# Pooling steps after the bounds and sums of h, the first sum of h in another place, one product ahead by one

## The reference

```
h      = gelu(x @ fc1_w.T + fc1_b)                  # 512 -> 2048
shared = h @ fc2_w.T + fc2_b                        # 2048 -> 384
expert = h @ experts_w[indices[b]].T + experts_b    # 2048 -> 128, weights chosen per batch
x      = x + concat(shared, expert)
scores = tanh(x @ W1 + b1) @ v
p      = softmax of the scores over the tokens that a mask (prefix, postfix or cloze) leaves
x      = x + (p @ x) / count
```

## Time and profile before

| what | value |
|---|---|
| median of 3 runs | 1432.12 us (1429.52 to 1435.58) |
| the profiled execution | 1433.8 us, of which its span 1431.7 us |
| PE busy | 1328.0 us (93%) |
| DVE busy | 1073.7 us (75%) |
| ACT busy | 968.6 us (68%) |
| POOL busy | 271.7 us (19%) |
| mean granted clock of PE | 0.971 |

### The profile page before, as it was taken

The page is one execution under the profiler, slowest core; times in us unless marked ns, Lnnn a source line. Parts: engine busy times, 40 slices in busy tenths (PEclk is TensorE's granted clock), DMA queues, the critical chain, the costliest instruction groups (busy, mean ns, idle before and its releaser), DMA issues.

```text
span 1431.7 us, 25597 instructions
## 1 busy us (share of the span) xinstructions
PE 1328.0 (93%) x9849; PEld 974.8 (68%) x9849; DVE 1073.7 (75%) x2092; ACT 968.6 (68%) x1764; POOL 271.7 (19%) x380
## 2 busy tenths in 40 slices
PE   9999999989989899898998989989899798997998
PEld 4457484757768577685776857768577685775855
DVE  7888897758678676786767867677676686766898
ACT  5769678575856758577685766857658476584772
POOL 0000101211222112221222212222221221122201
PEclk9999999999999999999999999999999999999999
DMA  7630223253352533534335343453434434335306
GB/s 276 190 83 15 46 82 67 67 125 75 97 110 71 121 81 97 104 82 111 81 99 102 84 108 82 108 96 83 109 79 110 91 86 105 82 96 104 69 17 118
DMA packets 73885, 136.43 MB, mean 95 GB/s; under 512 B 9747, under 2 KB 34211, under 8 KB 71331
## 3 DMA queue, kind: packets, MB, share of 16 engines
q0 software_dynamic: 28032, 56.63, 22.9%
q1 hardware_dynamic: 45154, 77.38, 16.4%
q10 hardware_dynamic: 576, 0.79, 0.2%
HBM read 45.65 MB, written 18.87 MB: 45 GB/s over the span
## 4 chain that ended last, share of the span: by engine, by line
PE 69%; DVE 16%; DMA 9%; ACT 3%; issue 2%; POOL 1%; POOLq 0%; DVEq 0%; ACTq 0%
PE ps L649 12%; PE ps L547 12%; PE ps L549 11%; PE ps L548 11%; DMA hl<-hl 8%; PE ps L657 4%; PE ps L660 4%; PE ps L636 3%; PE ps L638 3%; PE ps L637 3%; DVE xl L1619 2%; DVE hl L1662 1%; DVE hl L1619 1%; ACT L1199 1%; DVE space L2064 1%
## 5 line engine op out<-in xcount | busy, mean ns | idle before, releaser
L547 PE MATMUL ps<-xh,w1h 128*128 128x256 f16 x960 | 261.7, 273 | 0.0
L549 PE MATMUL ps<-xh,w1l 128*128 128x256 f16 x960 | 261.7, 273 | 0.0
L548 PE MATMUL ps<-xl,w1h 128*128 128x256 f16 x960 | 261.7, 273 | 0.0
L1035 ACT ACTIVATE g<-ps,b1s,ds 128x512 f32<-128x512 f32 x240 | 173.3, 773 | 65.5 <-PE ps L549 65.5
L547 PE MATMUL ps<-xh,ch 128*128 128x256 f16 x720 | 196.4, 273 | 0.0
L549 PE MATMUL ps<-xh,cl 128*128 128x256 f16 x720 | 196.2, 273 | 0.0
L548 PE MATMUL ps<-xl,ch 128*128 128x256 f16 x720 | 196.2, 273 | 0.0
L1619 DVE SCALAR_TENSOR_TENSOR hl<-g,ix,hh 128x512 f16<-128x512 f32 x243 | 176.1, 745 | 3.1
L1009 ACT ACTIVATE hh<-g,ix 128x512 f16<-128x512 f32 x243 | 161.6, 719 | 0.0
L1009 ACT ACTIVATE ps<-ps 128x256 f32<-128x256 f32 x192 | 71.3, 371 | 94.5 <-PE ps L660 57.0
L649 PE MATMUL ps<-hh,w 128*128 128x512 f16 x576 | 134.1, 379 | 0.0
(11 more groups left out here) (364 smaller groups left out, 3183.6 us busy)
## 6 DMA issues: line engine op xcount, KB each, us to landing
space<-in_xT SPq DMA_DIRECT2D x62, 256.0 KB, 3.2
g<-space SPq DMA_DIRECT2D x60, 256.0 KB, 3.5
er<-in_ew SPq DMA_DIRECT2D x15, 1024.0 KB, 4.9
out<-space SPq DMA_DIRECT2D x60, 256.0 KB, 3.2
space<-space POOLq DMA_DIRECT2D x52, 256.0 KB, 3.3
hl<-hl POOLq DMA_DIRECT2D x24, 512.0 KB, 7.7
g<-space POOLq DMA_DIRECT2D x30, 256.0 KB, 4.1
g<-g POOLq DMA_DIRECT2D x30, 256.0 KB, 3.3
```

What stands on the lines that cost most here:

```text
L547: mm(to, wh, mh, start=i in (1, 5) and c == 0, stop=False, skip_group_check=True)
L548: mm(to, wh, ml, start=False, stop=False, skip_group_check=True)
L549: m = mm(to, wl, mh, start=False, stop=c == 1, skip_group_check=True)
L1035: act(in_two(g_of(b, k)), src, ACT.Gelu, bias=b1s[:, k:k + 1], scale=ds1[:, b % 2, p:p + 1]).then_inc(gelu_done)
```

## The change

In `vector_program` the pooling steps of a paired batch are given out as 2, 3, 7, 3 and 2 instead of 9, 4 and 4. They follow `bounds`, `third_sum` and `batch_scales` with what hangs on them, instead of standing ahead. `first_sum` writes T1 to `h[1, FIRST]`, over T3, and leaves T2 as it is. So it waits for the expert's product 7 and no longer for the POOL transfers; product 5 reads the new place, and `split_x2_high`, which overwrites `h[1, SECOND]`, also waits for the expert's product 3. The static product 5 goes ahead of the expert's 3. `fourth_sums` moves into `sum_quarters`, ahead of the transfer into T4, and waits for the second sum alone. On ACT the split of T4 moves into the opening and `inverses` up by one. In the opening `product3` goes ahead of `score`. At the start SP's first puts wait for the low part of w2's second chunk.

```diff
-    H_OF = {1: (FIRST_K, 0), 6: (FIRST_K, 0), 5: (FIRST_K, 0), 7: (FIRST_K, 1),
+    H_OF = {1: (FIRST_K, 0), 6: (FIRST_K, 0), 5: (FIRST_K, 1), 7: (FIRST_K, 1),
...
-               (STATIC, 3), (EXPERT, 3), (STATIC, 5), (STATIC, 4), (EXPERT, 5), (EXPERT, 4))
+               (STATIC, 3), (STATIC, 5), (EXPERT, 3), (STATIC, 4), (EXPERT, 5), (EXPERT, 4))
...
         def sum7(b, v):
-            e.wait_ge(s_step, s_value(b, E3_DONE if v == EXPERT else T3_HIGH))
-            e.wait_ge(moved, t3_low_moved(b))
+            e.wait_ge(s_step, s_value(b, E3_DONE if v == EXPERT else T2_DONE))
...
+            sum5(b, STATIC)
             sum3(b, EXPERT)
-            sum5(b, STATIC)
...
+            product3(n, 0)
             score(b)
-            product3(n, 0)
...
         def split_x2_high(b, c):
+                e.wait_ge(s_done, nth_product(b, EXPERT, 3))
...
             split_x2_high(b, ROW)
+            split_x_high(n, T4)
             fifth_copy_of_sum(b, EXPERT)
...
+                inverses(b - 1)
                 third_of_sum(b, EXPERT)
-                inverses(b - 1)
                 split_x_high(b + 1, T2)
                 split_x_high(b + 1, X22)
-                split_x_high(b + 1, T4)
...
         def first_sum(b, h):
-            e.wait_ge(s_done, nth_product(b, EXPERT, 6))
-            e.wait_ge(moved, all_moved(b))
-            tt(y, y, x, ALU.subtract).then_inc(s_step)
+            e.wait_ge(s_done, nth_product(b, EXPERT, 7))
+            tt(h[:, 1, FIRST_K, :], y, x, ALU.subtract).then_inc(s_step)
...
                 expert_sum2(b)
-                pool(9)
+                pool(2)
                 bounds(b + 1)
                 third_sum(b)
+                pool(3)
                 second_sum(b, hh)
                 second_sum(b, hl)
                 batch_scales(b + 1)
                 expert_sum3(b)
                 add_left(b, STATIC)
                 add_left(b, EXPERT)
-                pool(4)
+                pool(7)
                 first_sum(b, hh)
                 first_sum(b, hl)
                 x_low(b + 1, X11)
                 x_low(b + 1, X21)
+                add_row(b, STATIC)
                 x_low(b + 1, T3)
                 x_low(b + 1, T1)
-                add_row(b, STATIC)
...
+                add_row2(b, EXPERT)
                 x2_low(b, ROW2)
-                add_row2(b, EXPERT)
                 add_first(b + 1, 0)
                 x2_low(b, 3)
+                x2_low(b, 0)
                 add_second(b + 1, 0)
-                x2_low(b, 0)
-                pool(4)
+                pool(3)
                 attention_low(b)
                 add_first(b + 1, 1)
+                pool(2)
...
+        e.wait_ge(w2l_done, nth_chunk(1, 3))
         put_quarters(1)
...
         def fourth_sums(b):
-            e.wait_ge(s_step, s_value(b, E2_DONE))
+            e.wait_ge(s_step, s_value(b, T2_DONE))
...
             add_quarters(b, T2, g[:, PLACES.index(T3), :])
+            if paired(b - 1):
+                fourth_sums(b - 1)
             e.wait_ge(*combined_by(b, T2))
             add_quarters(b, T4, g[:, PLACES.index(T2), :])
```

More of the change, by code:

```diff
@@ L2645, in fourth_sums @@
             e.wait_ge(s_done, nth_product(b, EXPERT, 2))
-            e.wait_ge(s_step, s_value(b, E2_DONE))
+            e.wait_ge(s_step, s_value(b, T2_DONE))
             eng.dma_start(ee[:, 1].rearrange("p a k n -> p (a k n)"),
                           expert_sums[b % 2][:, 1].rearrange("p a k n -> p (a k n)"), accum_op=ALU.add).then_inc(moved, 16)
-            e.wait_ge(s_step, s_value(b, T2_DONE))
             for h in (hh, hl):
@@ L2673, in gpsimd_program @@
             sum_quarters(n + 1)
-            if paired(n):
-                fourth_sums(n)
             mend(n - 1)
```

## The result

The changed kernel takes 1351.0 us, the median of 4 runs (1350.62 to 1351.38), against 1433.32 us for the kernel before (4 runs, 1429.52 to 1435.58): a ratio of 0.9428, 95% interval 0.9406 to 0.945. The forecast was 1356 within 1342 to 1384.

What follows compares the result with a forecast made beforehand. PE, busy 93% of the span, bounds the kernel, so its idle and slow time is the gain: 126.4 us removed less 50.6 new, net 75.8 off 1433.8, gives 1358.0, less 1.7 for the median: 1356 us, range 1342 to 1384.

Steps and rivals of the forecast that it cites:

- Part 1: PE's `mx` wait in paired batches: bounds ahead of seven pooling steps removes 61.8 us and 27.6 us of slow clock.
- Part 2: Second sum of h, late next: PE idles 1.5 us for hh and 0.25 for hl, 1.75 us a batch.
- Part 3: First sum, behind seven pooling steps: PE idles 1.5 us at static 5 and 0.25 at its low half.
- Part 4: POOL transfers into `hl`: 19.9 us of waits go, 5 come, including 0.2 a batch for T4's transfer.
- The 17 us that I put beside it: POOL transfers: loss if T4's transfer slowed those issued before it by a full 1.6 us a batch.
- Part 5: Opening: waits for the last row add and `attention_low` go, 13.5 us; 3.6 us of new wait for `keep_score`.
- the term for `keep_score`: Opening, score one product later: 0.25 to 0.3 us of new wait, 3.6 us in all.
- Part 6: Start, SP's four puts moved later: effect between -1.4 and +1.5 us, taken as 0.
- A: PE's corrections: new stalls lower the clock once a batch, 28 us more, 1384 us; chance 0.12.
- B: Expert 3: T4's transfer or the earlier start costs 1.6 us or more a batch, 1373 us; chance 0.12.
- C: ACT: T4's split delays the expert's fifth copy if its transfer lands past 603.6; slower, 1457 us at 612; chance 0.04.
- D: Chain product waits for something else, so 12 x 5.15 stay; within 7 us of 1432; chance 0.04.

Runs made afterwards that it cites:

- bounds-late kernel: The changed kernel with all nine pooling steps ahead of `bounds` again: 1398.83 us, ratio 0.976 to the kernel before.
- the fastest kernel: The changed kernel with both second sums before the exponentials' pooling step, four steps before the first sum, score before product 3, own semaphore for expert weights' transfer: 1302.67 us.
- the kernel with the old order: The changed kernel with expert product 3 ahead of static product 5 again, the first sum keeping its new place: 1391.32 us.
- the second sum ahead of the exponentials: The changed kernel with both second sums of h ahead of the pooling step that waits for ACT's exponentials: 1334.98 us.
- the kernel with T4's transfer first: The changed kernel with POOL's transfer into T4 of g ahead of the fourth sums again: 1351.82 us.
- bounds alone: The kernel before with only `bounds` moved, after two pooling steps with the other seven directly behind: 1398.82 us.
- bounds alone with the transfer held back: The kernel before with `bounds` moved ahead and the transfer of expert weights held until the second sum is done: 1425.71 us.
- the one with the old place and order: The changed kernel with the first sum over T2 again, waiting for all fourth-sum transfers, and expert product 3 ahead of static 5: 1393.23 us.

## Why the prediction was right

The answer was, the mechanism was, and the size was within 7 us, in part because errors cancelled. Point by point, by its parts.

**Part 1, bounds ahead: right.** `mx` was forecast ready four us before PE wants it, and is (558.53 against 562.51). The bounds-late kernel brings back exactly the 61.8 us. The slow clock went in full: 29.3 us by the granted clock over PE's busy time, where the sum had 27.6 + 3.6 = 31.2. It took batch 6's 2.3 us for all twelve stalls, and in batches 12 and 14 the slow stretch was half as long.

**Part 2, the second sum as the next late thing: right.** Forecast 1.5 and 0.25, measured 1.43 and 0.27. It is read off the same queue of DVE: the step that needs the exponentials, then the sum.

**Part 3, the first sum: right.** Forecast 1.5 and 0.25, measured 1.45 (0.52 in the last batch) and 0.27. Parts 2 and 3 together: 42 us forecast, 33.6 + 6.4 = 40.0 measured.

**Part 4, POOL's transfers: right in size, with one wrong step in it.** The wait is 1.6 us in three batches (0.19, 0.20 and 1.18), where 5 us stood in the sum, 2.4 of them a price for T4's transfer on the fourth sums (its "own run of about 1.6" stands in no row). The chain from the second sum to the landing takes 10.6 us in batch 6, as forecast. The price was zero, because the step that had T4 issued right behind the others was wrong: POOL held the transfer back for 7.66 us, until all of them had landed. The Trainium skill ("DMA: Bandwidth & Descriptors", "Issuing engines are not separate DMA queues") has all transfers share 16 engines and interleave. The 17 us that I put beside it did not come, and the changed kernel does not test the rule, since T4's transfer never ran beside the fourth sums. In the fastest kernel it does, which agrees with the rule, and there the late one pays: in batch 6 the fourth sums of hh and hl land 7.0 and 8.9 us after their issue in both kernels, while T4's takes 6.1 us instead of 3.5 (6.1 to 7.7 over the twelve batches, against 3.2 to 4.6). That the order of the products makes this cover was in the prediction ("thanks to static 5 going ahead"), but not what it is worth with the rest in place: 40 us.

**Part 5, the opening: mis-sized.** Both waits went, 13.5 us. The new gaps are 2 x 0.29 x 12 = 7.0 us, where the term for `keep_score` was 3.6: the step stopped at the first product that waits for `keep_score`, and left out ACT's next first copy, which stands behind it. It also left out what the removed wait was made of: in the attend part before there was a second gap of 0.21 us a batch, too short to be listed, 2.5 us in all, and it went too.

**Part 6, the start: 1.3 us gained,** inside its bounds of -1.4 to +1.5. Taking the wait away gives about 1 us back.

**The sum.** Ahead of each listed wait the last matmul counts as busy for 0.27 us, where the pace is 0.11: 0.16 us of tail each, for 46 waits before and 27 after, 3.1 us less. Removed 61.8 + 29.3 + 19.9 + 13.5 + 2.5, 1.3 at the start and 3.1 of tails are 131.4. New 33.6 (the listed stalls), 1.6 for the transfers, 7.0 in the opening and the 6.4 of low halves are 48.6. The difference is 82.8, and the spans differ by 82.1. Against the forecast of 75.8 the missing 7 us are 3.4 of transfers that cost nothing, 2.0 of smaller stalls, and 2.5, 1.3 and 3.1 not counted or taken as 0, less 1.9 of clock and 3.4 of a second gap. The lower bound of the range does not follow from the terms named for it: without T4's price (2.4) and half of the second and third parts' idle (21) the time is 1356 - 23, so 1333 and not 1342; for 1372 no working is given. The time measured lies in the range either way.

**The rivals.** *A, the new stalls keep the clock low:* not in the changed kernel. All 24 stalls (1.43 to 1.46 us, the last one 0.52) were followed by full pace. The rule of the Trainium skill that stood beside it ("TensorE: Matmul & The Clock Gate", "A second HAM failure mode: psum-queue depth-cycling") did not decide in this kernel. A was closer than its 0.12 sounded, however: in the kernel with the old order, the six waits of 2.31 to 2.65 us all lowered the clock, and with the second sum ahead of the exponentials two waits of 2.11 and 2.15 did. *B, POOL's transfers become the wait:* did not happen, yet the same kernel shows how near it was; with one product less of cover they are 36.1 us. *C, T4's split on ACT:* PE lost nothing by it, but one of the signs that the prediction named as wrong came: ACT waited for T4's transfer in its opening, in batches 3, 4 and 12 (0.88, 0.34 and 0.40 us). I had T4 issued at once, and it was held back by 7.66 us; against C I also gave 10.6 us as the slowest chain from the second sum to PE, which is batch 6's, where the slowest of before is 12.1. What was left is 1.45 us in batch 6, in which ACT waits for PE ahead of the fifth copy at 583.95, and 0.46 in batch 3. *D, it does not do what it says:* excluded by the `mx` rows. Its price was wrong: the bounds-late kernel keeps the whole stall with the rest of the change and takes 1398.83 us, and not 1432 within 7.

## What to carry to other kernels

When a stall is taken away, work out for every later consumer both times again: when the producer is done and when it is now wanted. Whoever forgets the second (as I did with the first sum, after the stall ahead of it went) sees the stall move on and not go. An edit can be worth nothing by itself and much together with another, as the free place with the product that may then go ahead: cost such pairs as a pair, and look for work that may run in the shadow of a transfer before trying to shorten the transfer. Gaps too short for the list of waits were found here by comparing row starts with the pace, and count twelve times all the same.

## What the runs showed of the hardware

**An issue that waits for earlier transfers.** POOL stood for 7.66 us ahead of issuing a 256 KB adding transfer, until the third of three 512 KB adding transfers had landed (POOL's rows of the changed kernel); in all twelve batches the issue starts 0.26 us after that landing. In the fastest kernel, where the first of the three signals another semaphore, the same issue stood for 2.57 us only, until that first one had landed (issued at 551.88, 4.9 us to landing, and the next issue at 557.07). Again the distance from that landing is 0.26 us in all twelve batches:

```profile
551.88 0.85 POOL L2653 DMA_DIRECT2D ee<-expertsums  x1 [3.80 <-DVE hl L1732]
...
557.07 0.87 POOL L2661 DMA_DIRECT2D g<-g  x1 [2.57 <-issue]
```

In the kernel with T4's transfer first, the issue of the fourth sum of hh stands for 1.29 us in batch 6 and comes 0.26 us after T4's has landed, with a single other transfer then in flight, where the changed kernel has three. So a plain limit on how many are in flight does not explain it. What holds the issue back was not settled: no run changes the number or size of the transfers by itself. For a plan it means that an adding transfer's place in POOL's order can delay it by the whole landing time of those ahead of it, and POOL's own next work with it.

**The clock after a stall does not follow from its length alone.** Waits of 5.1 us were followed by the 1.2 GHz level each time (48 of 48, in before, bounds late, bounds alone, and bounds alone with the transfer held back), those of 1.43 to 1.46 in the changed kernel never (23 of 23). Waits up to 1.96 us, the longest such in the kernel before, did not lower it in the corrections of any kernel here. Between 2 and 4 us it is mixed. With the second sum ahead of the exponentials, two of four waits of 2.11 to 2.15 us lowered it. With the old product order, the six of 2.31 to 2.65 us did, but one of 2.95 and one of 3.77 did not. In the kernel before, one of 3.14 did not while 2.39 and 3.08 did. Four windows, each right behind a wait (columns as above; the clock stands third from the end). The first two are both from batch 3 behind a wait of 2.93 us at the same product, in the kernel with the old order and in the one with the old place and order. The others are from the former, behind 3.77 and 3.79 us:

```profile
329.80:333.80 4.00, 3.93 (x21) 2.91 (x22) 0.99 (x2) 0.00 (x0) 1.86 (x5) 0.57 0.39 68
329.80:333.80 4.00, 4.00 (x37) 3.60 (x38) 3.69 (x4) 0.29 (x1) 3.32 (x4) 1.00 0.41 72
1188.50:1192.50 4.00, 3.98 (x37) 3.58 (x38) 0.10 (x1) 0.27 (x1) 1.87 (x5) 1.00 0.38 66
1101.90:1105.90 4.00, 3.99 (x24) 3.06 (x25) 0.08 (x1) 0.00 (x0) 1.86 (x5) 0.64 0.38 66
```

So in a kernel like this a plan may count on full pace after waits like those of up to 1.96 us and on a loss after 5, and should carry both for what lies between; what else decides is open.
